# A gated feed-forward in four units of four token tiles: its per-tile work, done in lumps or one tile a step

## The reference, cut to what matters

```python
def _layernorm(x, axis=-1, eps=1e-05):
    return (x - m) / jnp.sqrt(v + eps)

def _L0_ffn_ref(x, gate_up_packed, gate_up_scales, down_packed, down_scales):
    gate_up = jnp.einsum('bsh,oh->bso', x, w_gu)          # 512 -> 2 x 1408
    gate, up = (gate_up[..., :I], gate_up[..., I:])
    h = jax.nn.silu(gate) * up
    y = jnp.einsum('bsi,hi->bsh', h, w_down)              # 1408 -> 512
    rms = jnp.sqrt(jnp.mean(y * y, axis=-1, keepdims=True) + EPS)
    return y / rms

x = x + jnp.tanh(g_xattn[0]) * _L0_xattn_ref(_layernorm(x), ...)
x = x + jnp.tanh(g_ffn[0]) * _L0_ffn_ref(_layernorm(x), ...)
```

## Time and profile before

| | |
|---|---|
| median of 3 runs | 2760.99 us (2758.08 to 2767.07) |
| the profiled execution | 2759.97 us, span 2757.9 us |
| TensorE busy in the span | 2507.7 us (91%) |
| VectorE busy in the span | 1779.6 us (65%) |
| ScalarE, GpSimd busy | 1390.4 us (50%), 1033.5 us (37%) |
| first matmul of unit 0's `up` to the last add | 515.32 to 863.39 us |

### The profile page before, as it was taken

How to read it: one execution, slowest core, us unless ns; L and a number is a source line. 1 busy time by engine, 2 the same in 40 slices (tenths; PEclk the granted TensorE clock), 3 DMA queues, 4 the chain that set the end, 5 groups by cost and what they waited for, 6 DMA issues and landing times. The chain is left out here.

```text
span 2757.9 us, 46086 instructions
## 1 busy us (share of the span) xinstructions
PE 2507.7 (91%) x15884; PEld 1965.6 (71%) x15884; DVE 1779.6 (65%) x3774; ACT 1390.4 (50%) x3499; POOL 1033.5 (37%) x965
## 2 busy tenths in 40 slices
PE   7899997699997999998999999999999997299994
PEld 4666664467765788886888888888888886155552
DVE  6767698687876666665766666666667664622221
ACT  4777876455654444443655555555555553022221
POOL 3344321455554555554322222222222221055552
PEclk9999999899998999998999999999999998599997
DMA  3110121200103555557512522331141127599997
GB/s 138 50 47 22 44 65 49 86 1 31 54 31 117 196 181 185 198 178 249 163 47 65 158 74 63 113 97 43 55 151 52 44 78 240 165 301 298 298 297 164
DMA packets 220906, 337.05 MB, mean 122 GB/s; under 512 B 23556, under 2 KB 104836, under 8 KB 220164
## 3 DMA queue, kind: packets, MB, share of 16 engines
q1 hardware_dynamic: 203363, 290.70, 33.2%
q0 software_dynamic: 14912, 39.85, 6.3%
q10 hardware_dynamic: 2400, 3.55, 0.4%
HBM read 227.70 MB, written 110.53 MB: 123 GB/s over the span
## 5 line engine op out<-in xcount | busy, mean ns | idle before, releaser
L2150 POOL TENSOR_SCALAR a_prob<-a_prob,a_rinv 128x640 f32<-128x640 f32 (+3 forms) x256 | 253.7, 991 | 743.0 <-DVE a_rinv L2312 743.0
L2302 DVE TENSOR_REDUCE a_mx<-a_s_ps 128x1 f32<-128x640 f32 (+3 forms) x256 | 262.3, 1024 | 250.1 <-PE a_s_ps L2222 244.8
L2174 ACT ACTIVATE a_probT<-a_t_ps 128x512 fp32r<-128x512 f32 (+3 forms) x512 | 237.2, 515 | 350.1 <-PE a_t_ps L2230 350.1
L2318 DVE TENSOR_TENSOR a_probT<-a_t_ps,a_probT 128x512 fp32r<-128x512 f32 (+3 forms) x512 | 276.7, 582 | 44.7 <-ACT a_probT L2174 44.1
L2165 ACT ACTIVATE a_prob<-a_s_ps,a_nb,a_rs 128x640 f32<-128x640 f32 (+3 forms) x256 | 268.0, 1047 | 9.7 <-DVE a_nb L2303 9.7
L137 PE MATMUL a_o_ps<-a_probT,a_v 128*128 128x256 f32 x832 | 244.4, 294 | 0.0
L138 PE MATMUL a_o_ps<-a_probT,a_v 128*128 128x256 f32 x832 | 232.7, 280 | 0.0
L139 PE MATMUL a_o_ps<-a_probT,a_v 128*128 128x256 f32 x832 | 232.3, 279 | 0.0
L2230 PE MATMUL a_t_ps<-kept_ident,a_prob 128*128 128x128 f32 x1664 | 225.3, 274 | 2.6 <-POOL a_prob L2150 2.6
L2230 PEld LDWEIGHTS a_t_ps<-kept_ident,a_prob 128*128 128x128 f32 x1664 | 194.4, 141 | 25.7 <-POOL a_prob L2150 3.3
L716 PE MATMUL a_bank<-kept_ident,a_prob 128*128 128x128 f32 x1024 | 162.8, 288 | 41.7 <-ACT a_prob L574 31.3
(11 more groups left out here) (318 smaller groups left out, 6822.1 us busy)
## 6 DMA issues: line engine op xcount, KB each, us to landing
expert_ring<-in_w_gate SPq DMA_DIRECT2D x64, 384.0 KB, 19.2
expert_ring<-in_w_up SPq DMA_DIRECT2D x64, 384.0 KB, 21.3
expert_ring<-in_w_down SPq DMA_DIRECT2D x64, 384.0 KB, 24.3
l_q_hi<-p_turned SPq DMA_DIRECT2D x64, 256.0 KB, 2.4
l_q_lo<-p_turned SPq DMA_DIRECT2D x64, 256.0 KB, 2.1
h_split<-l_q_hi SPq DMA_DIRECT2D x62, 256.0 KB, 3.2
h_split<-l_q_lo SPq DMA_DIRECT2D x62, 256.0 KB, 3.8
l_v_hi<-p_vs SPq DMA_DIRECT2D x32, 256.0 KB, 2.3
```

The costliest lines, as they stand in the source:

```text
L2150: pool.tensor_scalar(prob[:, k % 4, 0:w], prob[:, k % 4, 0:w], rinv[:, k % 4:k % 4 + 1], 1.0, ALU.mult, ALU.mult).then_inc(s["weighted"], 1)
L2174: act.activation(probT[0][:, pair % 2, i * 4:i * 4 + n, k % 2], t_ps[i][:, 0:n * P].rearrange("p (m n) -> p m n", n=P), ACT.Copy).then_inc ...
L2302: step(dve.tensor_reduce(mx[:, k % 4:k % 4 + 1], s_ps[:, k % 2, 0:w], AX.X, ALU.max))
L2318: dve.tensor_tensor(probT[1][:, pair % 2, i * 4:i * 4 + n, k % 2], t_ps[i][:, 0:n * P].rearrange("p (m n) -> p m n", n=P), probT[0][:, pai ...
```

## The change

The work per tile is spread, tile t in one step: `add` in step 3 + t, statistics and the variance (one column) in step 5 + t, the root (one column) in step 6 + t, the turn in step 7 + t. `mean` and `rms` are done for two tiles at a time in steps 3 and 4, the squares for two in steps 2 and 3. `normalise` moves from VectorE to ScalarE, as an Identity with the scale 1/std and a bias `off` = -mean/std, which GpSimd makes. ScalarE takes `tanh` ahead of the turned tile and VectorE the turned tile behind everything else of the step. Loads and stores go by tile, each with a semaphore of its own. In unit 3 the two halves of a chunk of the next stage's weights go into two steps, 5 and 6, and 9 and 10.

```diff
     def load_rows(sp, x_in):
-        sp.dma_start(h["rows"][:], x_in.rearrange("(n t p) d -> n p t d", p=P, t=SUB)[0]).then_inc(h["loaded"][0], 16)
-
-    def statistics(dve, step, x, t0, t1):
-        if t0 == 0:
-            dve.wait_ge(h["loaded"][0], 16)
-        for t in range(t0, t1):
+        for t in range(SUB):
+            sp.dma_start(h["rows"][:, t], x_in.rearrange("(n p) d -> n p d", p=P)[t]).then_inc(h["loaded"][t], 16)
+
+    def statistics(dve, step, x, u, tiles):
+        for t in tiles:
+            dve.wait_ge(h["loaded"][t], 16 * (u + 1))
             step(dve.bn_stats(h["stats"][:, t], x[:, t]))
             step(dve.bn_aggr(h["mv"][:, t], h["stats"][:, t]))
-        if t1 == NT:
-            variance(dve)
-
-    def variance(dve):
-        dve.tensor_scalar(h["ve"][:], h["mv"][:, :, 1:2].rearrange("p t a -> p (t a)"), LN_EPS, None, ALU.add).then_inc(s["var_ready"], 1)
-
-    def root(pool, u):
-        pool.wait_ge(s["var_ready"], u + 1)
-        pool.tensor_tensor(h["rstd"][:], h["ve"][:], h["mhalf4"][:], ALU.pow).then_inc(s["rstd_ready"], 1)
+        variance(dve, tiles)
+
+    def variance(dve, tiles):
+        at = slice(tiles[0], tiles[-1] + 1)
+        dve.tensor_scalar(h["ve"][:, at], h["mv"][:, at, 1:2].rearrange("p t a -> p (t a)"), LN_EPS, None, ALU.add).then_inc(s["var_ready"], 1)
+
+    def root(pool, n, tiles):
+        at = slice(tiles[0], tiles[-1] + 1)
+        pool.wait_ge(s["var_ready"], n + 1)
+        pool.tensor_tensor(h["rstd"][:, at], h["ve"][:, at], h["mhalf4"][:, at], ALU.pow).then_inc(s["rstd_ready"], 1)
...
-TURN_STEPS = (9, 10)
+TURN_AT = 7
+NORM_AT = 6
+STAT_AT = 5
+ADD_AT = 3
...
-    return [(u + 1, 2 * TURN_STEPS.index(i) + t) for t in range(2)] if i in TURN_STEPS and u + 1 < UNITS else []
...
-                def load_x(u):
+                def load_x(u, t):
                     if u >= 2:
-                        sp.wait_ge(stored[u % 2], 16 * (u // 2))
-                    sp.dma_start(x[u % 2][:], x_src[u]).then_inc(loaded[u % 2], 16)
+                        sp.wait_ge(stored[t], 16 * (u - 1))
+                    sp.dma_start(x[u % 2][:, t], x_src[u * SUB + t]).then_inc(loaded[t], 16)
...
-                    sp.wait_ge(s["x_ready"], u + 1)
-                    sp.dma_start(x_dst[u], x[u % 2][:]).then_inc(stored[u % 2], 16)
-                    if u + 2 < UNITS:
-                        load_x(u + 2)
+                    for t in range(SUB):
+                        sp.wait_ge(s["x_ready"], u * SUB + t + 1)
+                        sp.dma_start(x_dst[u * SUB + t], x[u % 2][:, t]).then_inc(stored[t], 16)
+                        if u + 2 < UNITS:
+                            load_x(u + 2, t)
...
-                    if k < STEPS0 and u and i == 3:
-                        rms(u - 1, slice(0, SUB))
-                    if k < STEPS0 and i == 8:
-                        ffn["root"](pool, u + 1)
+                    if k < STEPS0 and u and i in (3, 4):
+                        rms(2 * (u - 1) + i - 3, slice(2 * (i - 3), 2 * (i - 3) + 2))
+                    if k < STEPS0 and u + 1 < UNITS and i >= NORM_AT and i < NORM_AT + SUB:
+                        t = i - NORM_AT
+                        ffn["root"](pool, 1 + u * SUB + t, (t,))
+                        pool.wait_ge(h["s"]["rstd_ready"], 2 + u * SUB + t)
+                        pool.tensor_scalar(off[:, t:t + 1], h["mv"][:, t, 0:1], h["rstd"][:, t:t + 1], -1.0,
+                                           ALU.mult, ALU.mult).then_inc(s["off_made"], 1)
...
+                def normalise(u, t):
+                    if u >= 2:
+                        act.wait_ge(s["x_ready"], (u - 2) * SUB + t + 1)
+                    act.wait_ge(s["off_made"], (u - 1) * SUB + t + 1)
+                    act.activation(yx[:, t], x[u % 2][:, t], ACT.Identity, bias=off[:, t:t + 1],
+                                   scale=h["rstd"][:, t:t + 1]).then_inc(s["normed"], 1)
...
+                    if k:
+                        tanh(k - 1)
                     for job in turned_behind(k):
                         turned_high(*job)
-                    if k:
-                        tanh(k - 1)
                     if u and i == 1:
                         copy_y(u - 1, 0)
                         copy_y(u - 1, 1)
-                    if u and i == 2:
-                        for t in range(SUB):
-                            square(u - 1, t)
+                    if u and i in (2, 3):
+                        square(u - 1, 2 * (i - 2))
+                        square(u - 1, 2 * (i - 2) + 1)
+                    if u + 1 < UNITS and NORM_AT <= i < NORM_AT + SUB:
+                        normalise(u + 1, i - NORM_AT)
                     if k:
                         high(k - 1)
                     if k in DOWN_HIGH_AT:
                         ffn["down_high"](act, DOWN_HIGH_AT[k])
-                    if u == UNITS - 1 and i in (5, 9):
-                        nxt["high"](act, (i - 5) // 4)
+                    if u == UNITS - 1 and i in (5, 6, 9, 10):
+                        nxt["high"](act, (i - 5) // 4, ((i - 5) % 4,))
...
-                        if r == 1 and u and i == 3:
-                            mean(u - 1, slice(0, SUB), u * SUB)
-                    for job in turned_behind(k):
-                        turned_low(*job)
+                        if r == 1 and u and i in (3, 4):
+                            mean(slice(2 * (i - 3), 2 * (i - 3) + 2), (u - 1) * SUB + 2 * (i - 3) + 2)
...
-                    if u and i in (3, 4):
-                        if i == 3:
+                    if u and ADD_AT <= i < ADD_AT + SUB:
+                        t = i - ADD_AT
+                        if t == 0:
                             dve.wait_ge(s["gated"], 1)
-                            dve.wait_ge(s["rms_ready"], u)
-                            step(dve.tensor_scalar(rg[:], rr[:], gate[:], None, ALU.mult))
-                        add(u - 1, (2 * (i - 3), 2 * (i - 3) + 1), lambda t: yx[:, t])
-                        if i == 4:
-                            dve.sem_inc(s["x_ready"], 1)
+                        if t in (0, 2):
+                            dve.wait_ge(s["rms_ready"], 2 * (u - 1) + t // 2 + 1)
+                            step(dve.tensor_scalar(rg[:, t:t + 2], rr[:, t:t + 2], gate[:], None, ALU.mult))
+                        add(u - 1, t, yx[:, t])
+                    for job in turned_behind(k):
+                        turned_low(*job)
                     if u + 1 < UNITS:
-                        if i in (6, 7):
-                            if i == 6:
-                                dve.wait_ge(loaded[(u + 1) % 2], 16 * ((u + 1) // 2 + 1))
-                            for t in (2 * (i - 6), 2 * (i - 6) + 1):
-                                step(dve.bn_stats(h["stats"][:, t], x[(u + 1) % 2][:, t]))
-                                step(dve.bn_aggr(h["mv"][:, t], h["stats"][:, t]))
+                        if STAT_AT <= i < STAT_AT + SUB:
+                            ffn["statistics"](dve, step, x[(u + 1) % 2], u + 1, (i - STAT_AT,))
+                    else:
                         if i == 7:
-                            ffn["variance"](dve)
-                        if i == 8:
-                            dve.wait_ge(h["s"]["rstd_ready"], u + 2)
-                            for t in range(SUB):
-                                normalise(u + 1, t)
-                    else:
-                        if i == 6:
                             dve.wait_ge(early["p_loaded"][0], 16)
                             step(dve.bn_stats(h["stats"][:, 0], early["x"][:, 0]))
                             step(dve.bn_aggr(h["mv"][:, 0], h["stats"][:, 0]))
-                            ffn["variance"](dve)
+                            ffn["variance"](dve, (0,))
                         if i == 8:
-                            dve.wait_ge(h["s"]["rstd_ready"], UNITS + 1)
+                            dve.wait_ge(h["s"]["rstd_ready"], 2 + (UNITS - 1) * SUB)
                             step(dve.tensor_scalar(nxt["first_normed"], early["x"][:, 0], h["mv"][:, 0, 0:1], h["rstd"][:, 0:1],
                                                    ALU.subtract, ALU.mult))
-                        if i in (5, 9):
-                            nxt["low"](dve, (i - 5) // 4)
+                        if i in (5, 6, 9, 10):
+                            nxt["low"](dve, (i - 5) // 4, ((i - 5) % 4,))
...
-    def high(act, ch):
-        for i in range(2):
+    def high(act, ch, halves=(0, 1)):
+        for i in halves:
...
-    def low(dve, ch):
-        for i in range(2):
+    def low(dve, ch, halves=(0, 1)):
+        for i in halves:
```

More of the change, by code:

```diff
@@ L525, in _ @@
                     if G == GROUPS0 + 3:
-                        ffn["root"](pool, 0)
+                        ffn["root"](pool, 0, range(NT))
             @block.scalar
@@ L926, in _ @@
                     if G == GROUPS0:
-                        ffn["statistics"](dve, step, h["rows"], 0, NT)
```

(8 more changed lines are left out.)

38 lines of the change are left out of this document (21 added, 17 removed).

## The result

| | before | changed |
|---|---|---|
| median | 2764.67 us (2758.08 to 2767.07, 5 runs) | 2737.05 us (2732.36 to 2743.61, 5 runs) |
| ratio | | 0.9903, 95% interval 0.9884 to 0.9923 |
| profiled execution, span | 2759.97, 2757.9 us | 2737.05, 2735.3 us |
| stage, first `up` to last `add` | 348.0 us | 326.9 us |
| units 0, 1, 2 | 85.1, 80.2, 79.1 | 79.0, 76.0, 76.1 |

The changed kernel is faster by 1.0%. The forecast was 2744 in a range of 2738 to 2752: the direction was right, the gain was larger than the range allowed, by 1 us. Of the 22.6 us between the two spans 21.1 lie in this stage; 17.0 had been forecast.

A forecast was written before the change was run, and what follows sets the result against it. The stage was taken as bound by TensorE, with only its idle time to win: 5.4 + 3.3 + 2.2 + 4.8 + 1.3 = 17.0 us off 2759.97 gives 2743.0, plus 1.0 for the median: 2744, range 2738 to 2752.

The forecast's parts named there:

- unit 3, steps 3 to 7: Unit 3: spreading the next stage's weight halves and the statistics brings 9.1 us over down to 4.3, a gain of 4.8.
- 74.8: Units 1 and 2: length in us without lateness, eleven undisturbed steps of 6.63 plus four turns of 0.465.
- the price of a half before r = 1: Unit 3, steps 6 and 7: ScalarE's half, then VectorE's held one, make r = 1 late by 1.45 us each.
- the second `mean` in step 4: Step 4: the 128x2 operation is held until GpSimd's first addition ends 3.15 us into the step, costing 0.7 us.
- the work counted against the 1.5 us: VectorE work behind `make`, counted from -0.23 us; beyond 1.5 TensorE waits: 0.4 in step 6, 0.2 in step 7 (units 1, 2).
- the stage's end: Unit 3 from step 10: last `down` but one at 10.1 instead of 12.87 us, 1.2 and 0.3 given back, gain 1.3.
- The rival in which it isn't held: Steps 3 and 4: the 128x2 `mean` doesn't wait for GpSimd, 6 x 0.7 us less, 2740; chance 0.05.
- The new chain: Rival: variance, root, `off` and Identity through three engines hold `high`, 0.45 us late in twelve steps, 2749.4; chance 0.12.
- Slack already used: Rival: the late evictions meet other delays, six steps at 1.3 us each, 2752; chance 0.06.
- nothing freed: Rival: the evictions of both engines stay as close as before, so no gain, 2760; chance 0.02.
- The slower one: Rival: a tile's store and load don't fit into 13.2 us, VectorE waits in eight tiles, 2776; chance 0.03.
- step 9's stall: Step 9: four `normalise` operations on VectorE take 3.85 us; moving them removes 1.95 in units 1, 2 and 4.85 in unit 0.

The follow-up runs named there:

- second pair: Kernel before and changed kernel each profiled once more with no edit: stages 348.6 and 327.0 us, medians 2758.88 and 2739.00 us.

## Why the prediction was right, and where it was wrong

The terms, forecast and measured, in the first pair of profiles and in the second:

| term | forecast | measured | second pair |
|---|---|---|---|
| unit 0 | 5.4 | 6.1 | 7.0 |
| unit 1 | 3.3 | 4.2 | 4.2 |
| unit 2 | 2.2 | 3.0 | 4.5 |
| unit 3, steps 3 to 7 | 4.8 | 5.4 | 3.3 |
| from step 10 to the last `add` | 1.3 | 2.4 | 2.6 |
| sum | 17.0 | 21.1 | 21.6 |

The measured columns differ by the kernel before, chiefly in step 9 of units 0 and 2 and in steps 5 and 6 of unit 3. What the forecast was to get right is the lengths after the change, and these repeat.

*What bounds the kernel* was right: what was won is TensorE's waiting, and the slow clock behind it. The changed units 1 and 2 are left with 1.2 and 1.3 us above 74.8.

*The price of the single operations* was right: 0.154 for the variance, 0.75 for `add`, and step 9 at 7.07 where 7.1 was forecast. So was the price of a half before r = 1: 1.43 and 1.36, forecast 1.45 each, with the clock at 1.00.

**The steps that failed are the sizes of three terms, and all erred the same way: the second `mean` in step 4, the work counted against the 1.5 us, and the stage's end.** For the `mean` I let both operations be held until "GpSimd's first addition ends 3.15 us into the step", and for the work I added the recorded length of each operation, with a hand-over. The timeline of unit 1 in the changed kernel, VectorE and then GpSimd; the steps begin at 616.21 (3), 623.46 (4), 630.38 (5), 637.01 (6) and 643.85 (7):

```profile
618.40 0.97 DVE L1448 TENSOR_SCALAR f_ms<-f_ss 128x2 f32<-128x2 f32 x1
...
622.86 0.22 DVE L1487 TENSOR_SCALAR f_rg<-f_rr,f_gate 128x2 f32<-128x2 f32 x1
...
625.66 0.65 DVE L1448 TENSOR_SCALAR f_ms<-f_ss 128x2 f32<-128x2 f32 x1
...
636.78 0.22 DVE L1487 TENSOR_SCALAR f_rg<-f_rr,f_gate 128x2 f32<-128x2 f32 x1
...
638.74 0.75 DVE L1434 SCALAR_TENSOR_TENSOR f_total<-f_bank,h_gs,f_total 128x512 f32<-128x512 f32 x1
...
643.62 0.74 DVE L1451 SCALAR_TENSOR_TENSOR hx_rows<-f_yx,f_rg,hx_rows 128x512 f32<-128x512 f32 x1
...
645.37 0.75 DVE L1434 SCALAR_TENSOR_TENSOR f_total<-f_bank,h_gs,f_total 128x512 f32<-128x512 f32 x1
```

```profile
618.06 2.53 POOL L1234 TENSOR_TENSOR f_total<-f_total,f_second 128x512 f32<-128x512 f32 x2
...
624.99 2.53 POOL L1234 TENSOR_TENSOR f_total<-f_total,f_second 128x512 f32<-128x512 f32 x2
```

*The mean in step 4.* Both means are held in the same way, until GpSimd's first addition is over (618.06 + 1.27 = 619.33, and 624.99 + 1.27 = 626.26). In step 3 that is 3.12 into the step, as forecast, and the step cost 0.62, forecast 0.7. By it TensorE reached step 4 late, while VectorE and GpSimd were delayed less: VectorE is behind `make` 0.60 us ahead of step 4 (622.86), where I had 0.23 throughout, and GpSimd's addition ends 2.80 into the step. So step 4 cost 0.29 (0.41 and 0.27 in units 2 and 3), forecast 0.7 again, 1.1 us in three units. The forecast of 1.0 to 1.3 us for a `mean` missed for the same reason: 0.97 and 0.65.

*The work in steps 6 and 7.* VectorE is 0.23 ahead there, just as I had it (637.01 - 636.78, 643.85 - 643.62). But the product, the `add` and a tile's statistics take 1.96 us from the first start to the eviction's (636.78 to 638.74), where I had 2.18, since an operation starts up to 0.09 before the recorded end of the one ahead; `add` and statistics take at most 1.75 (643.62 to 645.37), where I had 1.91. So the first eviction starts 1.73 and 1.52 into the step, and the steps cost 0.21 and nothing, forecast 0.4 and 0.2. With steps 3 and 4 that is the 0.9 of units 1 and 2. Unit 0 was 2.1 over, 2.8 forecast: its steps 6, 8 and 9 came 0.2, 0.1 and 0.2 below their terms. Its step 7 cost the forecast 0.6 by another cause than the forecast's: ScalarE's 128x1024 copy of the down weights (1.04) stands ahead of r = 0, and VectorE waited 0.16 for that eviction.

That the mean is held at all was forecast, and the runs show it for both widths: `mean` 0.771 in two columns and 0.145 in one, variance 0.631 and 0.154. The Trainium skill (VectorE: DVE Perf Modes, Mode 2×_2P) lets a width of 2 be split in halves for the two-port mode; the held operations fit it, though no row shows the mode itself. The rival in which it isn't held is out, though its time, 2740, was nearer than mine.

*The stage's end* failed by its own term. Windows, from step 10 to the resumption of `down`, from there to the last `down`, and to the last `add`; first the changed kernel, then the last two of before (the first is in the earlier trace rows):

```profile
818.44:828.35 9.91, 7.23 (x29) 4.91 (x27) 5.99 (x8) 6.09 (x9) 6.07 (x5) 1.00 0.16 53
828.35:835.10 6.75, 4.56 (x13) 3.08 (x13) 3.24 (x4) 2.67 (x4) 4.68 (x3) 0.75 0.24 79
835.10:844.16 9.06, 4.50 (x12) 3.03 (x12) 6.26 (x14) 3.24 (x9) 2.20 (x4) 0.76 0.59 203
```

```profile
848.10:853.88 5.78, 3.07 (x12) 2.17 (x12) 2.22 (x3) 2.66 (x4) 3.71 (x3) 1.00 0.00 1
853.88:863.34 9.46, 4.55 (x12) 3.06 (x12) 6.54 (x14) 3.25 (x9) 2.21 (x4) 0.74 0.35 111
```

9.91 was forecast as 10.1, from 12.87. The half before the last `make` then gave back 0.97 (6.75 - 5.78), not 1.5, and the tail was 0.4 shorter, which I had put at nothing: each of the last four adds now signals by itself, and they follow each other 1.72 us apart by the timeline, 1.85 before. That the signalling is the cause wasn't tested.

*The range.* With the right terms the sum against the profiled execution is 2738.9, and 2739.9 against the median shown, which is inside the range; that the median fell 1 us below it lies within the scatter of the runs, and the changed kernel's repeat, 2739.00, would have been inside. The forecast gain was 4 us too small either way. The range's low end, 2738, left no room for every term erring one way, nor for the runs: the changed kernel's medians were 2737.05 and 2739.00, those of before 2759.63 to 2765.04 in the four sets.

*The rivals.* The new chain doesn't hold `high` to any effect. In ten of the twelve steps it waits for `make` alone; in step 7 of units 1 and 2 it stands behind the Identity and is 0.1 us late (650.46 in unit 1), after `off` had been held, 0.78 us at 648.87. These steps last 7.06, like their neighbours. "Slack already used" and "nothing freed" are out by the units. The slower one is out by the transfers, which for a tile take less than half of the 13.2 us there are (DMA issues of the stage):

```profile
f_x<-x SPq DMA_DIRECT2D x8, 256.0 KB, 3.2
...
x<-f_x SPq DMA_DIRECT2D x8, 256.0 KB, 2.0
```

*What I had given the wrong weight.* The prediction put step 9's stall down to normalising on VectorE, and its end to the other engine. By the experiments the engine is worth 4.1 us, nearly all in unit 0, the halves 4.7, the adds one by one 3.2, and the narrow variance 3.2; these prices are each taken from the full change and don't add up to it, and the last is for a form that the kernel before didn't have. Normalising four tiles in one step in the changed kernel wasn't tried, since the turns stand in the same steps. Nor were the loads and stores by tile, the squares in two steps and the order of `tanh` and the turned tile tried by themselves.
